# A metaformer block on one core: the written order of five work tables and the places of the reciprocals are arranged anew

## The chip, the cores and the metric

One NeuronCore of a Trainium2 chip. The metric is device time in microseconds (us) of one execution, all weights and the eight images read from HBM and the result written back. Lower is better. The kernel before: 1431.96 us, the median of three runs (1431.75, 1431.96, 1438.49).

## The reference, cut to what matters

Eight images of 256 channels x 32 x 32, float32, pass one block: a channel norm, a multi-scale linear attention with a projection and batch norm added to the input, then a token norm and a mixture of six small experts added to that. The expert weights of an image are chosen from the mean of its tokens, so no expert product can be finished before the norm of the whole image is known.

```python
qkv = conv2d(ln_c(x), qkv_w)                       # 1x1, 256 -> 768
agg = conv2d(qkv, agg_dw_w, groups=768, padding=2) # depthwise 5x5
agg = conv2d(agg, agg_pw_w, groups=96)             # 8 by 8 groups
ms = concatenate([qkv, agg], axis=1)               # 64 heads of (q, k, v), 8 each
kv = einsum('bhnd,bhne->bhde', relu(k), [v, 1])
out = einsum('bhnd,bhde->bhne', relu(q), kv)
out = out[..., :-1] / (out[..., -1:] + 1e-15)      # the reciprocals meant here
x = x + bn(conv2d(out, proj_w))                    # 512 -> 256
t = ln_t(tokens(x))
w = experts(softmax(mean(t) @ router_w.T))         # top 2 of 11 rows
t = tokens(x) + sum_e w[e] * (gelu(t @ W1[e] + b1[e]) @ W2[e] + b2[e])
```

## The kernel before, in words

A list `ORDER` of 1786 work items is built by `schedule()` from tables of words. Each engine (PE, ACT, POOL, and SyncE for the transfers) walks the same list and executes its own part of each item, in that order; semaphores hold it until the other engines' parts are done. So the position of a word in a table is the program order of that step on every engine that has a part in it. `FIRST` is image 0 up to the keys of its second attention half, `SECOND` is image 1 with the second half of image 0 beside it, `PLAN` serves the next five images, `LAST` the eighth, `END` closes. In a word, the image number is relative: `-1` is the image before.

The items that matter here, with the line of their main instruction:

- `squares` (ACT, L781), `sums` (POOL, L913 and L915), `stats` (PE, L652; ACT copies it out), `rnorm` (POOL, ending in L929), `rbc` (PE L661, ACT L864), `apply` (POOL, L935), `high` (ACT), `low` (POOL, L940): one norm of an image, a chain in this order. Its third number is 0 for the channel norm and 1 for the token norm.
- `qkv` (PE L516, six fp16 products of 128x512; ACT L823 drains it), for six tiles of 128 rows and two halves.
- `diag` (PE L586, eight float32 products with diagonal matrices that ACT makes in `matrices`) and `b` (POOL, L983 adds what ACT L742 has scaled) share the depthwise 5x5 with VectorE (DVE). `b` takes the next waiting piece, if there is one.
- DVE doesn't walk the list. It runs the taps of the 5x5 (L1190) one behind the other, tile pair 1, then 2, then 0 of each image: 108 taps in image 0, 140 in image 1, 132 in the others. `AGG_PLACES` and `RAW_PLACES` say before which tap of an image it takes up a small task: the reciprocals of the attention sums (`rden`, L1074, raw half of this image, agg half of the last) and the routing of the experts.
- `tok` (PE transposes of q, k, v; ACT L844 and L845), `kv` (PE L616), `mask` (POOL, L947 and L948), `att` (PE L628, ACT L851 and L852), `scale` (POOL L956, after `rden`), `back` (PE L635), `proj` (PE L642, ACT, POOL L1010): the attention. `agg` (PE L596, L601) is the grouped 1x1 after the taps.
- `F` is a first expert product (`ffn`, PE L516, ACT L873 with the Gelu), `G` its split in two fp16 parts (ACT L767, L768; POOL L1024), `S` the second product (PE L534). There are 32 of each for every image, and they are given only when their inputs are in the list; else the word does nothing. `F` of an image can start when both `low` of its token norm are done.

All items with a PSUM product but `S` share two banks in turn: a product may be filled when the one two places before it in the list is drained by ACT. `qkv` of a tile pair overwrites the rows that DVE reads, so ACT drains it only when the taps of the image before are done for that pair.

Of the kernel before, what the change touches and what calls it, by code (L numbers as in the profile page):

```python
# [1253 lines left out]
```

## Time and profile before

| | us |
|---|---|
| median of three runs | 1431.96 |
| the profiled execution, its own time | 1438.11 |
| its span, first to last instruction | 1436.4 |
| PE busy in it | 1355.8 |
| DVE busy | 1198.0 |
| ACT busy | 1092.1 |
| POOL busy | 1043.6 |

The profiled execution stands at the upper one of the three timed runs. "Busy" of PE includes the stretches in which its clock was granted at half speed: there the same product takes twice as long. The first image is in flight alone up to about 171 us, the second with it up to about 331 us; from there each image takes 160 us up to the last two.

### The profile page before, as it was taken

Reading aid. Unit: us, or ns where it says so; the run is one execution under the profiler, and the core shown is the slowest. Engines: PE = TensorE matmul, PEld = TensorE weight load, DVE = VectorE, ACT = ScalarE, POOL = GpSimd, SP = SyncE. Lnnn points to the kernel's source line nnn. Section 1 sums busy time; section 2 is a strip of 40 time slices with the busy share of each in tenths; the row PEclk is TensorE's granted clock in tenths of the full one; section 3 lists DMA queues with packets and bytes.
Section 4 is the critical chain, followed back from the end, with each engine's and each line's share of the span. In section 5 each row is a group of like instructions: output and inputs, shape, how many; then the busy total and the mean of one; then the engine's idle time right before and its main releaser. Section 6 shows DMA issues by size and latency. Waiting matters only on the chain.

```text
span 1436.4 us, 18823 instructions
## 1 busy us (share of the span) xinstructions
PE 1355.8 (94%) x6844; PEld 771.8 (54%) x6844; DVE 1198.0 (83%) x1248; ACT 1092.1 (76%) x1919; POOL 1043.6 (73%) x771
## 2 busy tenths in 40 slices
...
GB/s 236 30 30 30 1 30 0 1 31 15 1 1 45 44 1 1 45 30 15 1 1 44 45 1 1 45 1 16 0 3 42 16 0 1 45 15 1 16 15 15
DMA packets 14284, 32.76 MB, mean 23 GB/s; under 512 B 2416, under 2 KB 5360, under 8 KB 13936
## 3 DMA queue, kind: packets, MB, share of 16 engines
...
q14 instruction: 38, 0.31, 0.1%
...
## 4 chain that ended last, share of the span: by engine, by line
PE 82%; ACT 9%; DVE 3%; POOL 2%; issue 2%; DMA 0%; ACTq 0%; DVEq 0%; SPq 0%; POOLq 0%
PE wbk L516 30%; PE acc L534 21%; PE wbk L642 7%; PE wbk L628 4%; PE wbk L601 4%; PE wbk L652 4%; PE wbk L616 4%; DVE dacc L1190 3%; PE wbk L586 3%; PE wbk L596 2%; PE wbk L635 2%; PE wbk L609 1%; ACT hb L873 1%; PE wbk L661 1%; ACT kt L851 1%
## 5 line engine op out<-in xcount | busy, mean ns | idle before, releaser
L1190 DVE SCALAR_TENSOR_TENSOR dacc<-qkvs,dww,dacc 128x930 f32<-128x930 f32 (+4 forms) x896 | 988.0, 1183 | 0.0
L1024 POOL TENSOR_TENSOR gl<-hb,gh 128x512 f16<-128x512 f32 x256 | 304.9, 1195 | 172.5 <-ACT hb L768 170.4
L983 POOL TENSOR_TENSOR dwo<-dwo,tapb 128x960 f32<-128x960 f32 (+2 forms) x136 | 307.4, 2261 | 75.7 <-ACT tapb L742 65.3
L873 ACT ACTIVATE hb<-wbk,b1s 128x512 f32<-128x512 f32 x256 | 174.4, 684 | 93.4 <-PE wbk L516 87.3
L534 PE MATMUL acc<-gh,w2h 128*128 128x512 f16 x512 | 194.1, 379 | 1.4 <-POOL gl L1024 1.0
L534 PE MATMUL acc<-gl,w2h 128*128 128x512 f16 x512 | 194.0, 379 | 0.0
L534 PE MATMUL acc<-gh,w2l 128*128 128x512 f16 x512 | 194.0, 379 | 0.0
L767 ACT ACTIVATE gh<-hb,ew 128x512 f16<-128x512 f32 x256 | 182.9, 715 | 0.1
L768 ACT ACTIVATE hb<-hb,ew 128x512 f32<-128x512 f32 x256 | 182.5, 713 | 0.0
L516 PE MATMUL wbk<-th,w1h 128*128 128x512 f16 x512 | 152.6, 380 | 4.9 <-POOL tl L940 1.7
L742 ACT ACTIVATE tapb<-qkvs,dww 128x1024 f32<-128x1024 f32 x136 | 154.0, 1146 | 1.7 <-POOL dwo L983 1.7
L516 PE MATMUL wbk<-th,w1l 128*128 128x512 f16 x512 | 152.8, 380 | 0.0
L516 PE MATMUL wbk<-tl,w1h 128*128 128x512 f16 x512 | 152.4, 379 | 0.0
L628 PE MATMUL wbk<-kvm,qr 128*128 128x144 f32 x512 | 83.6, 302 | 12.0 <-POOL kvm L948 3.0
L628 PEld LDWEIGHTS wbk<-kvm,qr 128*128 128x128 f32 x512 | 71.0, 193 | 30.8 <-ACT den L852 12.2
L1074 DVE RECIPROCAL den<-den 128x128 f32<-128x128 f32 x32 | 30.2, 945 | 64.9 <-ACT den L852 64.9
L823 ACT ACTIVATE qkvs<-wbk 128x512 f32<-128x512 f32 x96 | 56.6, 592 | 35.0 <-PE wbk L516 33.5
L516 PEld LDWEIGHTS wbk<-tl,w1h 128*128 128x128 f16 x512 | 50.1, 98 | 60.6 <-issue 0.3
L516 PEld LDWEIGHTS wbk<-th,w1l 128*128 128x128 f16 x512 | 50.2, 98 | 60.5 <-issue 0.2
L534 PEld LDWEIGHTS acc<-gh,w2l 128*128 128x128 f16 x512 | 50.1, 98 | 60.4
L534 PEld LDWEIGHTS acc<-gh,w2h 128*128 128x128 f16 x512 | 50.2, 98 | 58.0 <-issue 3.8
L956 POOL TENSOR_TENSOR kt<-kt,den 128x1024 f32<-128x1024 f32 x32 | 63.0, 1970 | 24.9 <-DVE den L1074 24.9
...
## 6 DMA issues: line engine op xcount, KB each, us to landing
...
```

The lines of the kernel that those rows point to most:

```text
L516: last = nc.tensor.matmul(dst, w[:, k, m * P:(m + 1) * P], d[:, k, c * CH:(c + 1) * CH], start=(i == 0), stop=(i == len(parts) - 1))
L534: last = nc.tensor.matmul(acc[:, m, :], w[:, t, m * P:(m + 1) * P], d[:, f % GB, :], start=(t == 0 and i == 0), stop=(t == FT - 1 and i == 2),
L628: last = nc.tensor.matmul(b[:, g * RD:(g + 1) * RD], qr[:, g, t * P:(t + 1) * P], kvm[:, g, :], start=True, stop=True)
L642: last = nc.tensor.matmul(b[:], wp[:, k, m * P:(m + 1) * P], (ac, qr)[k // CT][:, k % CT, c * CH:(c + 1) * CH], start=(k == 0), stop=(k == ...
L742: ins = nc.scalar.activation(tapb[:, BASE_NO[s, m, i] % 2, :], qkvs[:, m, :], ACT.Copy, scale=w)
L767: nc.scalar.activation(gh[:, f % GB, :], hb[:, f % GB, :], ACT.Copy, scale=w).then_inc(g_high, 1)
L768: nc.scalar.activation(hb[:, f % GB, :], hb[:, f % GB, :], ACT.Copy, scale=w).then_inc(g_scaled, 1)
L873: last = nc.scalar.activation(hb[:, f % GB, :], b[:], ACT.Gelu, bias=b1s[:, f % FT:f % FT + 1], scale=1.0 / (X_SCALE * W_SCALE))
L956: nc.gpsimd.tensor_tensor(v, v, r, ALU.mult).then_inc(att_scaled[h], 1)
L983: ins = nc.gpsimd.tensor_tensor(d3[:, oy, ox], d3[:, oy, ox], t3[:, iy, ix], ALU.add)
L1024: nc.gpsimd.tensor_tensor(gl[:, f % GB, :], hb[:, f % GB, :], gh[:, f % GB, :], ALU.subtract).then_inc(g_low, 1)
L1190: ins = nc.vector.scalar_tensor_tensor(out=dst[:, oy, ox], in0=i3[:, jy, jx], scalar=dww[:, m, tap:tap + 1], in1=a3[:, oy, ox], op0=ALU.mu ...
```

## The change

No instruction is added or removed: the 1786 items are the same ones, and only their positions in the list differ, and with them the order of each engine's program. The taps of DVE keep their order; five of the six small tasks in image 1 and some in the others move by one to six taps. The main moves:

- `FIRST`: the first `w1h` stands before the two drains of qkv tile 3; both drains of tile 4 stand before the matrices of tile 4, and both of tile 5 before the `w2h`. In image 2's first norm, `squares`, `sums` and `stats` stand before `agg.3.1` and the four qkv of image 1, `rnorm` right behind and `rbc` after those four (before, `squares` came between the qkv, and `stats` and `rbc` stood before the last of them). The second `apply` of it stands after the first qkv of tile 4 and not at the end of the table.
- `SECOND`: `high.1.0.1` stands after the second pair of proj; `squares.-1.1` and one `b` stand before `relu_q` and `qkv.1.2.0`; both `rbc` of the token norm after `att.5`; `qkv.1.3.0` among the `back`; one `G` between the first two `F`; `squares.2.0`, `sums.2.0` before the `agg` of tile 3; `stats.2.0` one `F` later.
- `RAW_PLACES[1]` goes from (66, 71) to (64, 68), that of the middle images from (64, 69) to (62, 66), `AGG_PLACES[1]` from (21, 23, 75, 78) to (20, 23, 73, 76).
- `PLAN`, `LAST` and `END` are shuffled over short distances; the number of `F`, `G` and `S` in each stage stays within one.

```diff
--- before.py
+++ after.py
@@ -163,77 +163,77 @@
 FIRST = """
 squares.0.0.0 squares.0.0.1 sums.0.0 wqh.0 stats.0.0 rnorm.0.0 roots.0 rbc.0.0.0 rbc.0.0.1 means.0.0
 means.0.1 means.0.2 means.0.3 apply.0.0.0 apply.0.0.1 high.0.0.0 low.0.0.0 high.0.0.1 low.0.0.1 qkv.0.2.0
-qkv.0.2.1 qkv.0.3.0 qkv.0.3.1 w1h.0.0 b w1l.0.0 qkv.0.4.0 matrices.0.4 qkv.0.4.1 qkv.0.5.0 w2h.0.0 w2h.0.1
-w2l.0.0 qkv.0.5.1 squares.1.0.0 matrices.0.5 w2l.0.1 w1h.0.1 b b diag.0.4.0 diag.0.4.1 w1l.0.1 squares.1.0.1
-sums.1.0 diag.0.5.0 diag.0.5.1 b qkv.0.0.0 b matrices.0.0 qkv.0.0.1 b matrices.0.1 stats.1.0 rnorm.1.0 b
-diag.0.0.0 qkv.0.1.0 rbc.1.0.0 rbc.1.0.1 b qkv.0.1.1 b diag.0.0.1 apply.1.0.0 apply.1.0.1 high.1.0.0 b
-diag.0.1.0 tok.0.0 b b tok.0.1 b b diag.0.1.1 b low.1.0.0 tok.0.2 tok.0.3 high.1.0.1 tok.0.4 b tok.0.5
-tok.0.6 tok.0.7 b relu_q.0.0 b kv.0.0.0 kv.0.0.1 mask.0.0 relu_q.0.1 att.0.0.0 att.0.0.1 b att.0.0.2
-att.0.0.3 scale.0.0.0 att.0.0.4 att.0.0.5 att.0.0.6 att.0.0.7 scale.0.0.1 back.0.0.0.0 back.0.0.0.1
-back.0.0.1.0 back.0.0.1.1 agg.0.2.0 agg.0.2.1 agg.0.3.0 b low.1.0.1 b agg.0.3.1 b qkv.1.2.0 squares.2.0.0
-squares.2.0.1 sums.2.0 qkv.1.2.1 qkv.1.3.0 stats.2.0 rnorm.2.0 rbc.2.0.0 rbc.2.0.1 qkv.1.3.1 agg.0.4.0
-agg.0.4.1 agg.0.5.0 apply.2.0.0 b agg.0.5.1 qkv.1.4.0 qkv.1.4.1 qkv.1.5.0 qkv.1.5.1 b b kv.0.1.0 kv.0.1.1 b
-mask.0.1 b b apply.2.0.1
+qkv.0.2.1 w1h.0.0 w1l.0.0 qkv.0.3.0 qkv.0.3.1 qkv.0.4.0 qkv.0.4.1 matrices.0.4 qkv.0.5.0 qkv.0.5.1 w2h.0.0
+w2h.0.1 w2l.0.0 matrices.0.5 w2l.0.1 w1h.0.1 diag.0.4.0 diag.0.4.1 squares.1.0.0 w1l.0.1 b squares.1.0.1 b b
+b sums.1.0 diag.0.5.0 b diag.0.5.1 qkv.0.0.0 matrices.0.0 b qkv.0.0.1 matrices.0.1 b stats.1.0 b diag.0.0.0
+diag.0.0.1 rnorm.1.0 rbc.1.0.0 b rbc.1.0.1 b apply.1.0.0 qkv.0.1.0 qkv.0.1.1 b b apply.1.0.1 high.1.0.0 b
+tok.0.0 diag.0.1.0 b b diag.0.1.1 tok.0.1 tok.0.2 low.1.0.0 high.1.0.1 tok.0.3 b b tok.0.4 tok.0.5 tok.0.6
+tok.0.7 b relu_q.0.0 kv.0.0.0 b kv.0.0.1 mask.0.0 relu_q.0.1 att.0.0.0 b att.0.0.1 b att.0.0.2 att.0.0.3
+scale.0.0.0 att.0.0.4 att.0.0.5 att.0.0.6 att.0.0.7 scale.0.0.1 back.0.0.0.0 back.0.0.0.1 back.0.0.1.0
+back.0.0.1.1 b agg.0.2.0 agg.0.2.1 agg.0.3.0 low.1.0.1 squares.2.0.0 squares.2.0.1 sums.2.0 stats.2.0
+agg.0.3.1 rnorm.2.0 qkv.1.2.0 qkv.1.2.1 qkv.1.3.0 qkv.1.3.1 rbc.2.0.0 rbc.2.0.1 b agg.0.4.0 agg.0.4.1
+apply.2.0.0 agg.0.5.0 agg.0.5.1 qkv.1.4.0 apply.2.0.1 qkv.1.4.1 qkv.1.5.0 qkv.1.5.1 b b kv.0.1.0 kv.0.1.1 b
+mask.0.1 b b
 """.split()
 
 SECOND = """
-agg.-1.0.0 G F agg.-1.0.1 agg.-1.1.0 S agg.-1.1.1 att.-1.1.0 S G b att.-1.1.1 att.-1.1.2 att.-1.1.3 S
-scale.-1.1.0 att.-1.1.4 F b qkv.0.0.0 G att.-1.1.5 S att.-1.1.6 att.-1.1.7 scale.-1.1.1 S qkv.0.0.1
-qkv.0.1.0 back.-1.1.0.0 G back.-1.1.0.1 back.-1.1.1.0 back.-1.1.1.1 qkv.0.1.1 b S proj.-1.0.0 proj.-1.0.1 b
-F high.1.0.0 low.1.0.0 high.1.0.1 proj.-1.1.0 proj.-1.1.1 F G low.1.0.1 b tok.0.0 tok.0.1 G F S tok.0.2
-tok.0.3 F tok.0.4 G tok.0.5 F b tok.0.6 tok.0.7 b b qkv.1.2.0 F relu_q.0.0 squares.-1.1.0 squares.-1.1.1
-kv.0.0.0 kv.0.0.1 sums.-1.1 b mask.0.0 relu_q.0.1 stats.-1.1 rnorm.-1.1 S att.0.0.0 G G b att.0.0.1
-att.0.0.2 G att.0.0.3 scale.0.0.0 rbc.-1.1.0 F S att.0.0.4 att.0.0.5 att.0.0.6 S rbc.-1.1.1 att.0.0.7
-apply.-1.1.0 apply.-1.1.1 qkv.1.2.1 scale.0.0.1 F high.-1.1.0 back.0.0.0.0 S back.0.0.0.1 G high.-1.1.1 b S
-back.0.0.1.0 F low.-1.1.0 low.-1.1.1 logits.-1 back.0.0.1.1 exp.-1 qkv.1.3.0 qkv.1.3.1 G agg.0.2.0 F F
-squares.2.0.0 F F agg.0.2.1 b squares.2.0.1 sums.2.0 agg.0.3.0 agg.0.3.1 G G S G stats.2.0 F rnorm.2.0 F G G
-S F S G b F agg.0.4.0 b S F S b G rbc.2.0.0 S G rbc.2.0.1 b apply.2.0.0 S F F S S G agg.0.4.1 G F agg.0.5.0
-S S G agg.0.5.1 qkv.1.4.0 b F b kv.0.1.0 F G G S G qkv.1.4.1 S b F S F G qkv.1.5.0 apply.2.0.1 qkv.1.5.1 S G
-b b F S F G G F S S G b F S kv.0.1.1 F mask.0.1 b G b S
+S G G F S agg.-1.0.0 agg.-1.0.1 agg.-1.1.0 agg.-1.1.1 att.-1.1.0 F b att.-1.1.1 att.-1.1.2 S att.-1.1.3 G S
+scale.-1.1.0 att.-1.1.4 att.-1.1.5 att.-1.1.6 b qkv.0.0.0 att.-1.1.7 qkv.0.0.1 F qkv.0.1.0 scale.-1.1.1 G
+back.-1.1.0.0 back.-1.1.0.1 back.-1.1.1.0 back.-1.1.1.1 F F proj.-1.0.0 S qkv.0.1.1 proj.-1.0.1 b high.1.0.0
+F b low.1.0.0 G proj.-1.1.0 proj.-1.1.1 high.1.0.1 low.1.0.1 G b G tok.0.0 tok.0.1 F tok.0.2 b S tok.0.3
+tok.0.4 b tok.0.5 S tok.0.6 tok.0.7 squares.-1.1.0 squares.-1.1.1 S b G relu_q.0.0 qkv.1.2.0 kv.0.0.0
+sums.-1.1 b F kv.0.0.1 mask.0.0 relu_q.0.1 stats.-1.1 rnorm.-1.1 b att.0.0.0 G S att.0.0.1 att.0.0.2 G
+att.0.0.3 scale.0.0.0 S att.0.0.4 att.0.0.5 rbc.-1.1.0 rbc.-1.1.1 apply.-1.1.0 att.0.0.6 att.0.0.7 S F G F F
+apply.-1.1.1 scale.0.0.1 qkv.1.2.1 back.0.0.0.0 high.-1.1.0 qkv.1.3.0 b back.0.0.0.1 high.-1.1.1 S G
+low.-1.1.0 low.-1.1.1 logits.-1 back.0.0.1.0 back.0.0.1.1 exp.-1 qkv.1.3.1 agg.0.2.0 F G S F F squares.2.0.0
+squares.2.0.1 sums.2.0 S agg.0.2.1 agg.0.3.0 agg.0.3.1 b F G G G F stats.2.0 G rnorm.2.0 S F F G F rbc.2.0.0
+agg.0.4.0 b S F S G b G S G rbc.2.0.1 b S F S agg.0.4.1 F G S agg.0.5.0 G F S G agg.0.5.1 qkv.1.4.0 F b S S
+F apply.2.0.0 b S b F G kv.0.1.0 b qkv.1.4.1 G G S qkv.1.5.0 F apply.2.0.1 G qkv.1.5.1 b S F F S b G G F S G
+b S kv.0.1.1 mask.0.1 F S F S G b b
 """.split()
 
 PLAN = """
-agg.-1.0.0 F agg.-1.0.1 S G agg.-1.1.0 agg.-1.1.1 S att.-1.1.0 att.-1.1.1 att.-1.1.2 F G qkv.0.0.0 qkv.0.0.1
-S G att.-1.1.3 scale.-1.1.0 att.-1.1.4 att.-1.1.5 att.-1.1.6 att.-1.1.7 scale.-1.1.1 qkv.0.1.0 b qkv.0.1.1
-high.1.0.0 F F back.-1.1.0.0 G S back.-1.1.0.1 F b back.-1.1.1.0 G b low.1.0.0 S back.-1.1.1.1 S proj.-1.0.0
-b b high.1.0.1 low.1.0.1 G proj.-1.0.1 proj.-1.1.0 F tok.0.0 tok.0.1 tok.0.2 tok.0.3 tok.0.4 tok.0.5 tok.0.6
-b b tok.0.7 b proj.-1.1.1 F relu_q.0.0 kv.0.0.0 squares.-1.1.0 squares.-1.1.1 sums.-1.1 kv.0.0.1 F mask.0.0
-relu_q.0.1 S G stats.-1.1 att.0.0.0 att.0.0.1 rnorm.-1.1 S G att.0.0.2 att.0.0.3 rbc.-1.1.0 rbc.-1.1.1
-apply.-1.1.0 G apply.-1.1.1 scale.0.0.0 att.0.0.4 F att.0.0.5 att.0.0.6 att.0.0.7 G qkv.1.2.0 scale.0.0.1
-high.-1.1.0 high.-1.1.1 S low.-1.1.0 F qkv.1.2.1 back.0.0.0.0 S b low.-1.1.1 logits.-1 back.0.0.0.1
...
+agg.-1.0.0 F agg.-1.0.1 agg.-1.1.0 agg.-1.1.1 G S att.-1.1.0 att.-1.1.1 att.-1.1.2 G F b qkv.0.0.0 S G
+qkv.0.0.1 att.-1.1.3 scale.-1.1.0 S att.-1.1.4 att.-1.1.5 att.-1.1.6 att.-1.1.7 scale.-1.1.1 b qkv.0.1.0 F
+qkv.0.1.1 high.1.0.0 F back.-1.1.0.0 G S back.-1.1.0.1 back.-1.1.1.0 b G S F S back.-1.1.1.1 G F low.1.0.0
+high.1.0.1 proj.-1.0.0 b proj.-1.0.1 b low.1.0.1 proj.-1.1.0 tok.0.0 tok.0.1 tok.0.2 tok.0.3 tok.0.4 tok.0.5
+tok.0.6 b tok.0.7 b proj.-1.1.1 F relu_q.0.0 kv.0.0.0 squares.-1.1.0 squares.-1.1.1 sums.-1.1 F kv.0.0.1 b
+mask.0.0 G relu_q.0.1 S stats.-1.1 rnorm.-1.1 att.0.0.0 att.0.0.1 S G att.0.0.2 att.0.0.3 rbc.-1.1.0
+rbc.-1.1.1 apply.-1.1.0 apply.-1.1.1 G scale.0.0.0 att.0.0.4 F att.0.0.5 att.0.0.6 att.0.0.7 scale.0.0.1 G
+high.-1.1.0 S qkv.1.2.0 high.-1.1.1 F qkv.1.2.1 back.0.0.0.0 b low.-1.1.0 low.-1.1.1 S logits.-1
...
-AGG_PLACES = {1: (21, 23, 75, 78), 2: (16, 18, 79, 85), 7: (22, 27, 84, 88), 8: (19, 21, 75, 83)}
-RAW_PLACES = {0: (82, 83), 1: (66, 71), 2: (64, 69), 7: (76, 78)}
+AGG_PLACES = {1: (20, 23, 73, 76), 2: (17, 18, 75, 85), 7: (19, 25, 85, 88), 8: (19, 21, 75, 83)}
+RAW_PLACES = {0: (82, 83), 1: (64, 68), 2: (62, 66), 7: (70, 76)}
```

## Rows read from the trace of the kernel before

**Rows 1.** The page: the span, and busy us, share and instructions per engine

```profile
span 1436.4 us, 18823 instructions
PE 1355.8 (94%) x6844; PEld 771.8 (54%) x6844; DVE 1198.0 (83%) x1248; ACT 1092.1 (76%) x1919; POOL 1043.6 (73%) x771
```

**Rows 2.** Windows: stretch, length, busy us per engine, PE clock, DMA share, GB/s

```profile
124.00:171.00 47.00, 38.43 (x233) 30.35 (x234) 42.97 (x44) 21.06 (x45) 18.26 (x15) 0.89 0.00 1
214.00:254.80 40.80, 26.86 (x158) 19.92 (x158) 40.33 (x50) 24.49 (x52) 34.16 (x23) 0.87 0.00 0
272.60:331.00 58.40, 57.33 (x297) 30.38 (x295) 58.40 (x56) 49.28 (x75) 48.23 (x35) 1.00 0.07 24
491.00:651.00 160.00, 158.27 (x837) 91.66 (x837) 150.36 (x156) 134.87 (x236) 130.56 (x97) 1.00 0.06 20
1131.00:1436.40 305.40, 288.26 (x1407) 151.70 (x1406) 145.42 (x167) 214.34 (x382) 174.10 (x138) 0.99 0.03 13
```

**Rows 3.** Waits of PE, 60 to 272.6 us: total us, times, longest

```profile
PE wbk L635 <- POOL kt L956: 9.0, 3, 5.5
...
PE wbk L661 <- POOL sv L929: 3.1, 1, 3.1
...
PE wbk L652 <- POOL rb L913: 2.7, 1, 2.7
```

**Rows 4.** The chain that ended last, 195 to 262 us: start, length, what

```profile
223.50 13.06 DVE dacc L1190 x12
236.56 0.86 DVE den L1074
...
237.49 1.97 POOL kt L956
239.46 4.39 POOL nrm L935 x2
...
244.05 1.97 POOL kt L956
...
246.16 1.09 PE wbk L635 x4
...
249.05 5.02 PE wbk L516 x12
...
257.64 2.76 PE wbk L516 x12
```

**Rows 5.** Timeline of DVE: start, us, operation, idle before and its releaser

```profile
130.09 0.95 DVE L1074 RECIPROCAL den<-den 128x128 f32<-128x128 f32 x1 [2.96 <-ACT den L852]
...
183.65 0.95 DVE L1074 RECIPROCAL den<-den 128x128 f32<-128x128 f32 x1 [0.70 <-ACT den L852]
...
187.62 0.95 DVE L1074 RECIPROCAL den<-den 128x128 f32<-128x128 f32 x1 [0.87 <-ACT den L852]
...
218.72 4.77 DVE L1179 SCALAR_TENSOR_TENSOR dacc<-qkvs,dww,dwo 128x1024 f32<-128x1024 f32 x2
...
319.99 3.60 DVE L1179 SCALAR_TENSOR_TENSOR dacc<-qkvs,dww,dwo 128x1024 f32<-128x1024 f32 x2
...
344.76 0.95 DVE L1074 RECIPROCAL den<-den 128x128 f32<-128x128 f32 x1 [5.86 <-ACT den L852]
```

**Rows 6.** Timeline of PE: starts of qkv.0.5.1, kv, the first F, agg.1.0.0

```profile
43.44 0.61 PE L516 MATMUL wbk<-xh,wqh 128*128 128x512 f16 x2 [1.33 <-ACT qkvs L823]
...
117.87 5.17 PE L616 MATMUL wbk<-vt,kt 128*128 128x129 f32 x32 [0.84 <-ACT vt L845]
...
254.79 0.59 PE L516 MATMUL wbk<-th,w1h 128*128 128x512 f16 x2
...
327.91 1.02 PE L596 MATMUL wbk<-dwo,pw 128*128 128x512 f32 x2
```

**Rows 7.** Timeline of POOL: the first sum of image 0's token norm, its two low

```profile
219.12 3.28 POOL L913 TENSOR_TENSOR rb<-yr 128x1024 f32<-128x1024 f32 x1
...
248.56 4.21 POOL L940 TENSOR_TENSOR tl<-nrm,th 128x1024 f16<-128x1024 f32 x2
```

More of the change, by code:

```diff
@@ new lines @@
+high.-1.1.0 S qkv.1.2.0 high.-1.1.1 F qkv.1.2.1 back.0.0.0.0 b low.-1.1.0 low.-1.1.1 S logits.-1
+back.0.0.0.1 back.0.0.1.0 G qkv.1.3.0 b F back.0.0.1.1 b S qkv.1.3.1 agg.0.2.0 agg.0.2.1 squares.2.0.0
+squares.2.0.1 agg.0.3.0 F S exp.-1 agg.0.3.1 F sums.2.0 S G G F G stats.2.0 F S b G F rnorm.2.0 F G S F F G
+S rbc.2.0.0 b G S agg.0.4.0 F b S agg.0.4.1 G S rbc.2.0.1 b F agg.0.5.0 S G G agg.0.5.1 G qkv.1.4.0 S F b F
+F apply.2.0.0 G S b qkv.1.4.1 qkv.1.5.0 G b S G F b S S F F G S G S apply.2.0.1 G F qkv.1.5.1 S G F F G b b
@@ L209 @@
+S G F S b kv.0.1.0 G S kv.0.1.1 b mask.0.1 F b S
 """.split()
 LAST = """
[L212 to L216 removed]
@@ L217 @@
-rnorm.-1.1 att.0.0.0 att.0.0.1 G b S F rbc.-1.1.0 F rbc.-1.1.1 apply.-1.1.0 apply.-1.1.1 G att.0.0.2 F
-att.0.0.3 scale.0.0.0 att.0.0.4 S att.0.0.5 att.0.0.6 att.0.0.7 high.-1.1.0 b S F high.-1.1.1 S F low.-1.1.0
-low.-1.1.1 logits.-1 G G F scale.0.0.1 back.0.0.0.0 G back.0.0.0.1 F b back.0.0.1.0 S back.0.0.1.1 agg.0.2.0
-S exp.-1 S b G agg.0.2.1 agg.0.3.0 F agg.0.3.1 G G G S F S G b b b F S S F S S G F G b G agg.0.4.0 F G S S F
-S G F F b agg.0.4.1 b agg.0.5.0 F G S G agg.0.5.1 S b G F S S G F F F G S S G F b F G S G S G kv.0.1.0
```

36 lines of the change are left out of this document (18 added, 18 removed).

## The prediction, made before the changed kernel ran

> **What bounds the kernel now.** First the page [rows 1]: PE is busy 1355.8 of 1436.4 us, so all its idle time is 80.6 us, and since the change keeps every instruction, that and the time lost at the half clock is all that there is to win. Then the windows [rows 2], for where the idle time lies. An image of the middle (491 to 651) takes 160.0 us with 1.73 us idle: no order gains more than that there. The two last images (1131 to 1436.4) hold 17.1 us. The stretch from 124 to 254.8 us is the soft one: 8.6 idle of 47.0 in 124 to 171, 13.9 of 40.8 in 214 to 254.8, and in both the granted clock is 0.89 and 0.87, a mix of 2.4 GHz and 1.2 GHz. From 272.6 on PE is nearly full (1.1 idle of 58.4), with expert products to fill every hole. So the end is the moment at which PE becomes full, plus a fixed amount of PE work: what brings image 0's token norm, and with it the first F at 254.79 [rows 6], forward, brings the end forward.
>
> Then the waits of PE in that stretch [rows 3]: 9.0 us for the scaled attention (L635 from POOL L956, one of 5.5), 3.1 for a norm factor (L661), 2.7 for a sum (L652). And the chain that ended last [rows 4], to see what is behind them: it runs over the taps of DVE (1.09 us each: 13.06 over 12), then the reciprocal at 236.56, POOL's scale at 237.49, its two apply (4.39), its second scale at 244.05, and PE's back at 246.16. That is, POOL waits for a reciprocal that stands behind taps, and the apply and the second scale queue behind the first. After it PE runs twelve products of qkv in 5.02 us at half clock where twelve F products take 2.76 a little later, and DVE has no idle time between 188.5 and 339 us but its small tasks.
>
> **The change part by part.** The sum is for the profiled execution: 1438.11 us, its span 1436.4 and 1.7 around it. It stands 6.15 above the median.
>
> *FIRST, up to kv.0.0.* `w1h` (1.9 us of ACT) now lies in ACT's wait for the qkv of tile 3, both drains of tiles 4 and 5 precede longer work, so the 1.33 us wait of qkv.0.5.1 [rows 6] and a smaller one go. PE is about 2.3 us ahead into the `diag`; of that ACT takes back some at the eight `tok`, which it drains at over 0.5 us each with a `high` and two `b` among them. I get kv.0.0 at 116.2 instead of 117.87 [rows 6]: 1.65 us. Ends: 0 (ACT's `b` eat all) and 2.5. DVE gains the same, because its first reciprocal waited 2.96 us for the attention [rows 5]; if nothing were gained before, it would still wait that.
>
> *Image 2's first norm.* `stats` and `rbc` now lie around four qkv (5.2 us of PE at full clock), which covers `rnorm`, so the 3.1 us wait for L929 [rows 3] and half a us before it go. In its place `stats` stands ahead of `agg.3.1`, and its second half needs POOL's second sum, which needs both `squares`, which ACT now does behind the drain of `agg.3.0`. I walk that to a wait of about 3.1 us. Net 0.5 gained; ends -1 and 3, the latter if the half clock that lies on `rbc` and qkv there (0.89 in the window) moves off too. The second `apply` (2.37 us of POOL) moves into a long idle time of POOL, and no longer stands between `b` and `scale`; it was covered there, so 0.
>
> *SECOND, to the first scale.* The reciprocals of image 0's second half waited 0.70 and 0.87 us [rows 5], so one place earlier costs DVE nothing as long as PE moves forward with it, and may save those two waits: DVE is 2.1 to 3.2 us ahead after them. `squares` off the drain of qkv.1.2.0, which waits for taps, gives ACT back 1.4 us and starts them 8 us earlier, but POOL's sum at 219.12 [rows 7] was queued behind four `b`, of which one now has to wait for the `squares`; I put the sum at 217 and the second sum 3 us ahead. Then the deciding edit: `RAW_PLACES[1]` 66 to 64 takes two taps, 2.2 us, out of the chain in front of the first scale, and 71 to 68 three out of the second. With DVE's own 2.1 to 3.2 that makes 4.3 to 5.4 us on POOL's scale at 237.49. What is late next is the attention product: its fourth drain, 3 us ahead as well, gets there at about 229.3, which allows up to 7.2. I take 6. Both `rbc` are one and two `att` later, and the `apply` still fit between the two scales. So back.1 and logits come 6 us sooner, and POOL's two `low` end at 246.5 instead of 252.77 [rows 7].
>
> One place where the page and the trace can be put side by side: DVE's two first taps of a tile pair (L1179, two inputs in SBUF) took 4.77 us [rows 5] while POOL's sum took 3.28 [rows 7], against 2.5 and 2.4 elsewhere. The Trainium skill (SBUF — State Buffer, "Who interferes with whom") has it that a DVE instruction with two SBUF inputs and a GpSimd one that reads SBUF lock each other out of a shared port. By that the later sum against the earlier taps would part them, and DVE would have 2.3 us more; the sum above does without.
>
> *To the first F and after.* Before, the first F came 2.0 us after `low`, behind four qkv groups' worth of products at half clock (5.02, [rows 4]). Now qkv.1.3.0 fills the wait for the second scale and only one qkv and one agg remain behind logits, so F starts with `low`: 246.5 against 254.79, a gain of 8.3, that is, 6.0 and 2.3 more. Then the 2.7 us wait of `stats` for POOL's sum [rows 3], which stood behind a `b`, goes; in its place ACT has a G before the second F's Gelu and two `squares` before it can drain `agg.2.1`, on which `agg.3.1` waits; I count about 2.2 lost again. Net 0.5; ends -2 and 3. Sum so far: 8.3 + 0.5 = 8.8 us (the 1.65 and 0.5 of the first parts are in the 6).
>
> *Does DVE allow it?* agg.1.0.0 starts at 327.91 [rows 6], its taps are done where DVE begins the next image, at 319.99 [rows 5]: 7.9 us of slack. PE moves 8.8 and DVE at least 2, so about 1 or more is left. DVE's next wait (5.86, [rows 5]) absorbs the difference. If DVE gained nothing, 7.9 would be the cap.
>
> *PLAN, LAST, END.* Short shuffles, with places of reciprocals moved by up to six taps. The rows bound them: below by 1.73 us idle per image of the middle, five of them, and about 12 of the last 17.1 us (over 4 are the drain and the store at the end). Upward, one new wait like those of the first images (0.7 to 3.1) per image would cost 3 to 15. The number of F in LAST is one less ahead of its token norm. I take 0.
>
> Sum: 8.8 us. 1438.11 - 8.8 = 1429.3 for such an execution. The runs at 1431.8 may lack a part of the half-clock time that the profiled one has; of the 5.02 us above, 2.3 would be missing there. For the median I take 8 us: 1424.0.
>
> The other side of the clock: in 214 to 254.8 it was granted at 0.87 with 13.9 us idle, and the products behind the idle time ran at 1.2 GHz. After the change PE still idles some 6 us in front of the first F. The Trainium skill (TensorE: Matmul & The Clock Gate, "What's actually happening") says that the clock is halved after an idle window and given back after a busy one. By that the half clock stays and lies on F, which nothing hides.
>
> **The rivals.** (a) *The half clock falls on F.* For: the wait before F doesn't vanish. The same length of slow products as before (5.02 us) moves to F; the 2.3 us that I gain there is gone: 5.5 to 6.5 us, 1426. (b) *The gain before PE is full is used up by DVE.* The waits of the reciprocals only move: DVE is dense, and if FIRST gives nothing and the first two places wait 1.1 us longer each, scale.0 comes 2.2 us sooner and no more. Against: 2.96 us of wait in image 0 are PE's doing. 3 us gained: 1429. (c) *The tables of the middle lose it.* PLAN runs five times; one new wait of 2 to 3 us in it (a `kv` that now stands at the very end, its mask straight before the next image's `att`) costs 10 to 15, and with 8 gained it turns the sign from 1.6 us per image on: slower by 4, 1436. Against: the order in the rest of PLAN is close to the old one, and ACT (134.9 of 160) and POOL (130.6) have room [rows 2]. (d) *LAST and END gain too.* 17.1 us idle; a third of it, 5, makes 1419.
>
> **How the numbers follow.** Forecast 0.45, (a) 0.15, (b) 0.12, (c) 0.10, (d) 0.18. The forecast's own range is 1420 to 1427. With (a), (b) and (d) whole and half of (c), the range is 1415 to 1433. A half per cent is 7.2 us, about what a measurement of this kernel tells from no change: faster means under 1424.8. (d) is, the forecast is to some seven tenths (its centre is 0.8 under the line), a tenth of the rest: 0.18 + 0.31 + 0.03 = 0.52. Slower than 1439.1 takes more than (c) in its middle: 0.06. The rest, 0.42, is within.
>
> **What would show it.** Reciprocal of image 1 (L1074) at about 230 instead of 236.5 and no 5.5 us wait of L635 behind it; the first F at 245 to 248; the wait for L929 at 151 us gone and one for L915 or L781 in its place; kv.0.0 near 116; windows of 160 us in the middle unchanged. Wrong if F starts before 249 and the span doesn't follow, or if an image of the middle takes over 161 us.

## The result, and the profile after

The changed kernel took 1422.66 us, the median of five runs (1418.52 to 1424.02), beside 1431.96 for the kernel before: ratio 0.9913, 95% interval 0.9886 to 0.9940. Timed again later beside more runs of the kernel before, it was 0.9903 (0.9875 to 0.9930). The forecast was 1424.0, range 1415 to 1433. The total came out; its parts did not, and that is what the experiments are about.

One thing must be known to read the numbers: the executions of the kernel before fall into two groups, near 1432 (clock mostly 0.990 to 0.992 over the span) and near 1438.7 (0.985 to 0.988). In the series of e1 to e4 below, 14 of its 35 runs were in the lower one. The profiles of before and after are both of the kind with more half clock (0.986 each), so they differ by 14.1 us where the first medians differ by 9.3.

The page of the kernel after, its answer to [rows 1]:

```profile
span 1422.3 us, 18823 instructions
PE 1350.7 (95%) x6844; PEld 775.6 (55%) x6844; DVE 1197.5 (84%) x1248; ACT 1091.6 (77%) x1919; POOL 1038.3 (73%) x771
```

Its windows (columns as in [rows 2]):

```profile
124.00:171.00 47.00, 39.49 (x234) 32.27 (x235) 40.20 (x40) 21.29 (x46) 20.00 (x16) 0.85 0.07 23
214.00:254.80 40.80, 31.63 (x198) 22.53 (x197) 39.87 (x54) 31.13 (x62) 34.90 (x24) 0.96 0.00 0
272.60:331.00 58.40, 57.32 (x286) 30.12 (x286) 58.40 (x53) 48.22 (x73) 46.78 (x34) 0.99 0.07 28
```

In 214 to 254.8, PE is busy 31.6 us instead of 26.9: there the early gain is. In 124 to 171 the clock is even lower than before, 0.85, and DVE is busy 40.2 instead of 43.0. The places where PE passes the first product of `agg.s.0.0` (L596), and the starts of kv.0.0 and of the first F, read from both timelines, say what each stage gave between these two executions:

| start of | before | after | gained so far |
|---|---|---|---|
| kv.0.0 | 117.87 | 114.48 | 3.4 |
| agg.0.0.0 | 170.82 | 170.40 | 0.4 |
| first F | 254.79 | 248.49 | 6.3 |
| agg.1.0.0 | 327.91 | 323.11 | 4.8 |
| agg.2.0.0 | 488.60 | 483.42 | 5.2 |
| agg.5.0.0 | 968.77 | 961.61 | 7.2 |
| the end | 1436.4 | 1422.3 | 14.1 |

So a third of it comes before 331 us, not all; 2.4 us in the stages of the middle and 6.9 from 969 on. The rows before 331 us hold for these two executions only. A second profile of the same changed kernel (e5 below, 1418.94 us) has agg.0.0.0 at 162.38, the first F at 245.01 and agg.1.0.0 at 317.85, 8.0, 3.5 and 5.3 us ahead of the first one. Behind agg.1.0.0 the two agree: 1099.2 and 1099.4 us to the end, where the kernel before takes 1108.5. So 9.3 us of the gain lie there in both, and it is the opening that differs from one execution to the next.

The waits of PE from 60 to 272.6 us, the answer to [rows 3]:

```profile
PE wbk L609 <- ACT vt L845: 6.9, 7, 2.0
PE wbk L628 <- POOL kvm L948: 3.9, 1, 3.9
PE wbk L652 <- POOL nrm L915: 3.4, 2, 3.2
PE wbk L665 <- ACT th L752: 2.9, 1, 2.9
PE wbk L601 <- DVE dwo L1173: 2.7, 1, 2.7
```

The 5.5 us for the second scale and the wait for L929 have gone; the one for the second sum (3.2) has come as forecast, and two are new, 2.9 in front of logits and 2.7 for DVE's taps. The largest sum, the waits of `tok` for ACT's drains (L609), was 4.0 before. DVE's timeline:

```profile
129.83 0.95 DVE L1074 RECIPROCAL den<-den 128x128 f32<-128x128 f32 x1 [5.64 <-ACT den L852]
...
182.89 0.95 DVE L1074 RECIPROCAL den<-den 128x128 f32<-128x128 f32 x1 [1.20 <-ACT den L852]
...
218.09 2.49 DVE L1179 SCALAR_TENSOR_TENSOR dacc<-qkvs,dww,dwo 128x1024 f32<-128x1024 f32 x2
...
231.89 0.95 DVE L1074 RECIPROCAL den<-den 128x128 f32<-128x128 f32 x1 [0.43 <-ACT den L852]
...
342.35 0.95 DVE L1074 RECIPROCAL den<-den 128x128 f32<-128x128 f32 x1 [1.05 <-ACT den L852]
```

The first wait grew from 2.96 to 5.64, so DVE gained 0.3 us there and not 1.65; the 5.86 of slack at 339 is nearly used up. The two first taps of the tile pair at 218 us took 2.49 us instead of 4.77: POOL's sum, which ran beside them before, now starts at 219.91, when they are nearly done. POOL's timeline from 219 to 249, the answer to [rows 4, 7]:

```profile
219.91 2.89 POOL L913 TENSOR_TENSOR rb<-yr 128x1024 f32<-128x1024 f32 x1
...
231.26 2.30 POOL L983 TENSOR_TENSOR dwo<-dwo,tapb 128x992 f32<-128x992 f32 x1
233.52 1.97 POOL L956 TENSOR_TENSOR kt<-kt,den 128x1024 f32<-128x1024 f32 x1
235.44 4.68 POOL L935 TENSOR_TENSOR nrm<-yr,rb 128x1024 f32<-128x1024 f32 x2
240.07 1.97 POOL L956 TENSOR_TENSOR kt<-kt,den 128x1024 f32<-128x1024 f32 x1
244.17 4.21 POOL L940 TENSOR_TENSOR tl<-nrm,th 128x1024 f16<-128x1024 f32 x2
```

Both scales come 4.0 us sooner, though the sum comes 0.8 later. The first reciprocal is done at 232.84, and the scale then stands behind a `b` (L983) to 233.5: 0.7 us of what DVE gained is lost there. Two `low` end at 248.4 and F follows at 248.49.

### The profile page after: what moved, and what is told of

Same layout as the page of the kernel before. It is cut to its first block, busy times and chain, and to the rows that moved or that the text cites. A ratio compares the mean times of both kernels' runs of the same rounds, so it can differ in the third digit from the quotient of the medians.

```text
span 1422.3 us, 18823 instructions
## 1 busy us (share of the span) xinstructions
PE 1350.7 (95%) x6844; PEld 775.6 (55%) x6844; DVE 1197.5 (84%) x1248; ACT 1091.6 (77%) x1919; POOL 1038.3 (73%) x771
## 4 chain that ended last, share of the span: by engine, by line
PE 82%; ACT 9%; POOL 3%; DVE 3%; issue 2%; DMA 0%; DVEq 0%; SPq 0%; ACTq 0%; POOLq 0%
PE wbk L516 28%; PE acc L534 21%; PE wbk L642 8%; PE wbk L628 4%; PE wbk L601 4%; PE wbk L616 4%; PE wbk L586 4%; PE wbk L652 3%; DVE dacc L1190 2%; PE wbk L596 2%; PE wbk L635 1%; PE wbk L609 1%; ACT kt L851 1%; PE wbk L661 1%; POOL gl L1024 1%
## 5 line engine op out<-in xcount | busy, mean ns | idle before, releaser
L1190 DVE SCALAR_TENSOR_TENSOR dacc<-qkvs,dww,dacc 128x930 f32<-128x930 f32 (+4 forms) x896 | 988.0, 1183 | 0.0
L1024 POOL TENSOR_TENSOR gl<-hb,gh 128x512 f16<-128x512 f32 x256 | 300.3, 1175 | 176.7 <-ACT hb L768 174.1
L983 POOL TENSOR_TENSOR dwo<-dwo,tapb 128x960 f32<-128x960 f32 (+2 forms) x136 | 307.7, 2262 | 46.8 <-ACT tapb L742 41.6
L873 ACT ACTIVATE hb<-wbk,b1s 128x512 f32<-128x512 f32 x256 | 174.3, 684 | 81.9 <-PE wbk L516 75.4
L534 PE MATMUL acc<-gh,w2h 128*128 128x512 f16 x512 | 194.3, 380 | 1.8 <-POOL gl L1024 1.0
L534 PE MATMUL acc<-gl,w2h 128*128 128x512 f16 x512 | 194.3, 379 | 0.0
L534 PE MATMUL acc<-gh,w2l 128*128 128x512 f16 x512 | 194.2, 379 | 0.0
L516 PE MATMUL wbk<-th,w1h 128*128 128x512 f16 x512 | 152.4, 379 | 3.1 <-ACT hb L873 1.4
L516 PE MATMUL wbk<-tl,w1h 128*128 128x512 f16 x512 | 152.3, 379 | 0.0
L516 PE MATMUL wbk<-th,w1l 128*128 128x512 f16 x512 | 152.3, 379 | 0.0
L534 PEld LDWEIGHTS acc<-gh,w2l 128*128 128x128 f16 x512 | 50.1, 98 | 60.5 <-issue 0.3
L516 PEld LDWEIGHTS wbk<-tl,w1h 128*128 128x128 f16 x512 | 50.1, 98 | 60.4
L516 PEld LDWEIGHTS wbk<-th,w1l 128*128 128x128 f16 x512 | 50.1, 98 | 60.4
L534 PEld LDWEIGHTS acc<-gh,w2h 128*128 128x128 f16 x512 | 50.3, 98 | 55.8 <-issue 3.2
L534 PEld LDWEIGHTS acc<-gl,w2h 128*128 128x128 f16 x512 | 50.1, 98 | 53.5 <-issue 2.5
```

What stands on the lines that cost most here:

```text
L516: last = nc.tensor.matmul(dst, w[:, k, m * P:(m + 1) * P], d[:, k, c * CH:(c + 1) * CH], start=(i == 0), stop=(i == len(parts) - 1))
L534: last = nc.tensor.matmul(acc[:, m, :], w[:, t, m * P:(m + 1) * P], d[:, f % GB, :], start=(t == 0 and i == 0), stop=(t == FT - 1 and i == 2),
L873: last = nc.scalar.activation(hb[:, f % GB, :], b[:], ACT.Gelu, bias=b1s[:, f % FT:f % FT + 1], scale=1.0 / (X_SCALE * W_SCALE))
L983: ins = nc.gpsimd.tensor_tensor(d3[:, oy, ox], d3[:, oy, ox], t3[:, iy, ix], ALU.add)
L1024: nc.gpsimd.tensor_tensor(gl[:, f % GB, :], hb[:, f % GB, :], gh[:, f % GB, :], ALU.subtract).then_inc(g_low, 1)
L1190: ins = nc.vector.scalar_tensor_tensor(out=dst[:, oy, ox], in0=i3[:, jy, jx], scalar=dww[:, m, tap:tap + 1], in1=a3[:, oy, ox], op0=ALU.mu ...
```

## The experiments

### One table at a time (e1 to e4)

Each is the kernel before with one part of the change, the words exactly those of the diff (here only the names of what is taken over):

```diff
 e1: +FIRST     e2: +SECOND, +AGG_PLACES[1], +RAW_PLACES[1]
 e3: +PLAN, +AGG_PLACES[2], +RAW_PLACES[2]     e4: +LAST, +END, +AGG_PLACES[7], +RAW_PLACES[7]
```

> The kernel before with the new FIRST alone. Theory A (the prediction's): the attention of image 0 comes 1.65 us sooner and image 2's first norm saves half a us more; DVE goes with it, so about 2 us are gained in the end, 1430. Theory B (read from the two traces, agg.0.0.0 at 170.8 before and 170.4 after): the 3.4 us that kv.0.0 comes sooner are lost again in the wait for the mask (3.9 us) and in half clock before 171 us, so 0 to 0.5 us are gained, 1432.

> The kernel before with the new SECOND and the places of image 1 alone. Theory A: the larger part of the forecast's 8.8 us is here, 6 to 7 us, 1425 to 1426. Theory B: of the 6.3 us by which the first F comes sooner, 1.5 are lost again behind it (a wait of 2.7 us of agg.1.4.0 for the taps of DVE), so 4 to 4.5 us, 1427.5; agg.1.0.0 starts at about 323.5.

> The kernel before with the new PLAN and the places of the images 2 to 6 alone. Theory A: 0 us (1432). Theory B: the step from agg to agg of an image goes from 160.05 to 159.4 us, five images, about 2.8 us, 1429. Rival C: the new PLAN gains only where SECOND hands over earlier, and alone its steps stay at 160.0.

> The kernel before with the new LAST and END and the places of the images 7 and 8 alone. Theory A: 0 us. Theory B: 157.2 + 154.6 us from agg.6.0.0 to the end become about 150.9 + 151.8, of which 2.6 are work that the new PLAN has done before; so 5 to 6.5 us, 1426 to 1427: most of what the change gains beside SECOND, and a part for which the prediction had put 0.

| kernel | ratio to before | 95% interval | median us, 12 runs |
|---|---|---|---|
| e1, FIRST | 0.9978 | 0.9959 to 0.9997 | 1434.22 |
| e2, SECOND | 0.9956 | 0.9935 to 0.9976 | 1430.93 |
| e3, PLAN | 0.9975 | 0.9953 to 0.9997 | 1429.98 |
| e4, LAST and END | 0.9950 | 0.9931 to 0.9970 | 1428.61 |

(before: 1437.19, 35 runs.) A median of the kernel before depends on how many runs fall in each group, so read the ratios. Each part gains by itself, e1 and e3 only just clear of 1. For e1 (0.22 per cent, about 3 us) the interval takes in theory A's 2 us and not theory B's 0 to 0.5. For e2 (0.44, about 6) it takes in both theories. Theory A gave 0 to the last two, and is wrong there: together they are over half. Theory B said 2.8 us for e3 and 5 to 6.5 for e4; the traces show 2.6 and 6.6 behind agg.1.0.0. In e3 the steps of the middle (from one image's first agg product to the next one's) are 159.40 us, as in the whole change, also behind the old SECOND; so rival C falls. The same stretch in both kernels, agg.2.0.0 to agg.3.0.0, first e3:

```profile
482.50:641.90 159.40, 157.71 (x837) 92.05 (x837) 150.14 (x155) 134.46 (x238) 130.26 (x97) 1.00 0.06 21
```

and the kernel before:

```profile
488.60:648.70 160.10, 158.37 (x838) 91.76 (x837) 150.46 (x157) 134.96 (x237) 130.66 (x97) 1.00 0.06 20
```

PE's idle time is the same 1.7 us; it is the busy time that fell by 0.66. The gain is in how closely the products follow each other, which the bound from idle time (1.73 per image) did not look at. The idle weight-load time put down to issue in front of L516 and L534 fell from 2.8 to 1.7 us; why just these orders do so stays open.

In e4 the steps from agg.5 to the end are 158.4, 150.9 and 151.8 (before: 155.8, 157.2, 154.6). The waits of PE in LAST, first of the kernel before, 1124 to 1282 us:

```profile
PE wbk L516 <- POOL tl L940: 1.7, 1, 1.7
PE wbk L616 <- ACT vt L845: 1.5, 1, 1.5
PE wbk L516 <- ACT kt L838: 1.0, 1, 1.0
PE wbk L661 <- ACT hb L873: 0.8, 1, 0.8
```

and of e4, 1119 to 1271 us:

```profile
PE wbk L516 <- ACT hb L873: 1.1, 2, 0.7
PE wbk L516 <- POOL tl L940: 0.8, 1, 0.8
PE wbk L628 <- ACT qr L836: 0.8, 1, 0.8
```

Three waits of 1.5, 1.0 and 0.8 us go and the one for `low` halves; 1.1 us for Gelu drains (L873) come. The kernel before has a half clock stretch of 3.4 us behind its wait for `low`, in 1196 to 1216 (mean granted clock there 0.91), and e4 has none. That stretch isn't in every execution of the old LAST: e1, e2, e6 and e7 have the same wait at full clock and a step of 156.1 instead of 157.2. So some 1.1 of the 6.6 us that e4's trace gains behind agg.1.0.0 is the clock, and 5.5 the order. With e3's 2.6 the 6.6 make 9.2, the 9.3 us of the whole change behind agg.1.0.0: these two parts add up.

e1's timeline has agg.0.0.0 at 166.49, 4.3 us before the kernel before, and e3 and e4, whose FIRST and SECOND are the old ones, have agg.1.0.0 at 322.2 and 320.4 instead of 327.9. So one execution cannot tell a gain of this size in the first 330 us: the same order lands up to 7.5 us apart. In 100 to 141 us the granted clock was 0.88 in the profile of before and 1.00 in those of e3 and e4. Only like can be set beside like: with more half clock agg.1.0.0 goes from 327.91 to 323.11 (4.8 us); with little of it, from 322.2 and 320.4 (e3, e4) to 317.85 (e5), 2.5 to 4.4 us. For kv.0.0 the mean of the six profiles with the new FIRST is 115.3, of the seven with the old one 116.9: 1.5 us, not the 3.4 of the table above.

### The whole again, the places, and the waits filled (e5 to e8)

e5 is the changed kernel again. e6 is e2 without its places. e7 is the kernel before with the places alone:

```diff
-AGG_PLACES = {1: (21, 23, 75, 78), ...
-RAW_PLACES = {..., 1: (66, 71), ...
+AGG_PLACES = {1: (20, 23, 73, 76), ...
+RAW_PLACES = {..., 1: (64, 68), ...
```

e8 is the changed kernel and, on PE, in front of four items:

```diff
+            FILLERS = {('att', 0, 0, 0): 12, ('back', 0, 0, 1, 0): 6, ('kv', 0, 0, 0): 2, ('logits', 0): 12}
...
+                    for i in range(FILLERS[it]):
+                        nc.tensor.matmul(acc[:, 0, :], w1h[:, 0, 0:P], w1h[:, 0, 0:CH], start=True, stop=True,
+                                         skip_group_check=True)
```

> The changed kernel itself, timed in the same series as the parts: the runs of the kernel before fall into two groups here, near 1432 and 1438.7, and its first five runs were nearly all of the lower one. Theory A (the prediction's 8 to 9 us, all before 331 us): 0.9940. Theory B (the parts add up: FIRST 0.2, SECOND 0.4, PLAN 0.25, LAST and END 0.5 per cent): about 0.987 to 0.988, 1424 where before is 1437.

> The kernel before with the new SECOND, but the places of the reciprocals of image 1 left as they were. Theory A: the places are the deciding edit of SECOND, scale.1.0.0 waits for the reciprocal behind tap 66 again, and 2 to 4 of SECOND's 6 us go: 0.997 to 0.9985. Theory B: the order of PE and ACT does it, 0.996 as with the places.

> The kernel before with the places of image 1 alone (RAW 64, 68; AGG 20, 23, 73, 76), all tables old. Theory A: the first scale comes about 2 us sooner, the second 2 to 3, back.1 with it, 2 us gained: 0.9985. Theory B: without the order that lets the attention product come sooner the reciprocal only waits: 0 (1.000).

> The changed kernel with 32 products more on PE that nothing reads (fp16, 128x512 into the still unused acc), put into four waits of image 0 and its token norm: 12 before att.0.0.0, 6 before back.0.0.1.0, 2 before kv.0.0.0, 12 before logits.0, 7 us of PE at full clock. Theory D: the two groups of times come from stretches at 1.2 GHz that follow PE's waits before 250 us; work in the waits holds 2.4 GHz, so the upper group goes and the median falls 2 to 4 us below the changed kernel's. Theory E: the groups have another cause, or the filling delays what it stands before: the same as the changed kernel or up to 5 us slower.

| kernel | ratio to before | 95% interval | median us (runs) |
|---|---|---|---|
| e5, the change | 0.9903 | 0.9875 to 0.9930 | 1421.59 (6) |
| e6, SECOND, old places | 0.9966 | 0.9947 to 0.9986 | 1431.67 (12) |
| e7, places alone | 0.9976 | 0.9953 to 0.9998 | 1430.79 (12) |
| e8, the change, waits filled | 0.9879 | 0.9851 to 0.9907 | 1416.48 (6) |

(before: 1437.33, 23 runs.) e5 lies between the two theories: theory A's 0.9940 is outside its interval, theory B's 0.988 inside. The places gain 0.24 per cent with all tables old, 3.4 us; the interval takes in theory A's 2 and ends just below 1. The traces speak more clearly against theory B, that the reciprocal would only wait. In e3, whose first two images are those of the kernel before, and e7 the first reciprocal of image 0 stands at 125.95 and 126.17, the clock is 1.00 up to 141 us in both, and then e7 has the scales of image 1 at 229.61 and 236.15 instead of 231.78 and 238.34, 2.2 us sooner each, which is two taps, and agg.1.0.0 1.5 sooner. SECOND's order without them gains 0.34, with them 0.44; the last two intervals overlap, so how much they add to it isn't told. The chain of [rows 4] was read rightly. The parts multiply to 0.986 and the whole is 0.990: the parts overlap by some 6 us, or less: 0.986 lies just below the whole's interval, and each part is known to 0.002 only.

e8 is the fastest kernel here, by work that nobody reads: 5 us under the changed one by the medians, 3.3 by the means of six runs each. Five of its runs lie in 1416.0 to 1418.2 and one at 1422.67, so the slower kind of execution became rarer and did not go.

### Why two groups, and where the early gain ends (e9 to e11)

e9 moves one word in SECOND of the changed kernel:

```diff
-agg.0.4.0 b S F S G b G S G rbc.2.0.1 ...
+b S F S agg.0.4.0 G b G S G rbc.2.0.1 ...
```

e10 is the kernel before with `FILLERS = {('att', 0, 0, 0): 12, ('back', 0, 0, 1, 0): 6, ('kv', 0, 0, 0): 2, ('back', 1, 0, 1, 0): 20}`. e11 is e8 with e9's word moved and `('stats', 2, 0): 12, ('agg', 0, 1, 0): 10` besides.

> The changed kernel with one word of SECOND moved: agg.0.4.0 (for image 1, agg.1.4.0) stands two products of F and S later, behind the piece b S F S. In the changed kernel PE waits 2.7 us at this word for the taps of DVE. Theory B: that wait is part of where the early gain goes; it shrinks to nothing and the kernel gains 1 to 2.7 us, agg.1.0.0 sooner by as much. Rival: DVE is what bounds this stretch, the wait comes back at the next thing that needs its taps (agg.1.4.1, the qkv of tile 4), 0 us.

> The kernel before, all tables and places old, with 40 products more on PE that nothing reads, in the same four waits of image 0 and its token norm (12 before att.0.0.0, 6 before back.0.0.1.0, 2 before kv.0.0.0, 20 before back.1.0.1.0). Theory D: the two groups of the kernel before (1432 and 1438.7) are the half clock between 115 and 140 us and its consequences; the upper group disappears, the median is 1429 to 1432, 0.994 to 0.996. Theory E: two groups as before, ratio 1.000 or above.

> The changed kernel with agg.0.4.0 later and the filling products of e8, and 22 more of them (12 before stats.2.0, where PE waits 3 us for the second sum, 10 before agg.0.1.0, where it waits 2.5 for ACT). Theory D with B: both gains add, 1413 to 1416, 2 us under e8, and the half clock at 141 and 168 us goes. Rival: these two waits lie beside DVE's taps and aren't on the path, and the filling delays them: as e8, 1416.5, or 1 us above.

The series of e9 to e11 has 17 runs of the kernel before, median 1432.63. e10: 0.9969 (0.9951 to 0.9987), median 1431.22, and its 12 runs lie between 1428.84 and 1433.41; of the 17 runs beside it, 8 were at 1437.2 and above. The upper group is gone, the lower one hardly faster: theory D, though its 0.994 to 0.996 was a little more than was found. The stretch 100 to 141 us, first the kernel before as profiled:

```profile
100.00:141.00 41.00, 30.97 (x151) 23.21 (x150) 36.97 (x37) 23.10 (x51) 29.00 (x18) 0.88 0.16 52
```

the kernel after:

```profile
100.00:141.00 41.00, 30.10 (x142) 24.38 (x141) 34.20 (x34) 20.24 (x47) 26.79 (x16) 0.79 0.15 52
```

and e10:

```profile
100.00:141.00 41.00, 36.01 (x198) 24.42 (x197) 39.15 (x39) 26.23 (x56) 27.09 (x17) 0.96 0.15 52
```

The same stretch in e5, which is the same program as the kernel after:

```profile
100.00:141.00 41.00, 28.83 (x168) 22.01 (x167) 39.43 (x38) 23.58 (x51) 27.86 (x17) 0.96 0.15 52
```

PE's rows say what happens, first the kernel before, then the kernel after:

```profile
126.08 6.51 PE L628 MATMUL wbk<-kvm,qr 128*128 128x144 f32 x32 [3.04 <-POOL kvm L948]
```

```profile
114.48 6.77 PE L616 MATMUL wbk<-vt,kt 128*128 128x129 f32 x32 [0.85 <-ACT vt L845]
125.11 7.32 PE L628 MATMUL wbk<-kvm,qr 128*128 128x144 f32 x32 [3.86 <-POOL kvm L948]
```

then e5, with its first reciprocal:

```profile
115.02 5.38 PE L616 MATMUL wbk<-vt,kt 128*128 128x129 f32 x32 [0.85 <-ACT vt L845]
122.41 5.18 PE L628 MATMUL wbk<-kvm,qr 128*128 128x144 f32 x32 [2.00 <-POOL kvm L948]
125.49 0.95 DVE L1074 RECIPROCAL den<-den 128x128 f32<-128x128 f32 x1 [0.91 <-ACT den L852]
```

and e3, the old opening with the clock at 1.00:

```profile
116.79 3.81 PE L616 MATMUL wbk<-vt,kt 128*128 128x129 f32 x32 [0.84 <-ACT vt L845]
122.62 5.17 PE L628 MATMUL wbk<-kvm,qr 128*128 128x144 f32 x32 [2.02 <-POOL kvm L948]
```

The clock falls to 1.2 GHz a first time in front of the mask, at `kv`, behind PE's short waits for ACT's drains at `tok` (0.50 in 114 to 120 us of the kernel after). What the slow kv sets off is told by the four short pieces of the mask on POOL (L947, L948) and DVE's two first taps of the next tile pair (L1179):

| profile | mask on POOL | it takes | DVE's two taps start | PE's wait for the mask | att |
|---|---|---|---|---|---|
| before | 123.54 | 2.4 | 124.62 | 3.04 | 6.51 |
| after | 121.75 | 3.3 | 121.50 | 3.86 | 7.32 |
| e5 | 120.90 | 1.4 | 122.05 | 2.00 | 5.18 |
| e3 | 121.10 | 1.4 | 123.55 | 2.02 | 5.17 |

Where a piece of the mask starts with these taps running it takes 1.1 to 1.4 us instead of 0.3 to 0.5. That is so in before, after, e1, e2, e6 and e9, and there the att products run in half clock for most of their time (6.2 to 7.4 us). In e3, e4, e5, e7, e8, e10 and e11 the last piece starts ahead of the taps, in e5 by 0.03 us, and att takes 5.1 to 5.2. So a small delay at kv decides between two times that lie far apart: the mask meets the taps, PE waits longer for it, the clock falls again, the reciprocals come later, and DVE, which has no slack before 339, loses for good what it waits: the fourth figure of the windows is its busy time, 37.0, 34.2 and 39.2 of 41 us, and 39.4 in e5. From before to e3 this can be added up. DVE's waits for the attention sums up to 190 us are 5.6 and 0.9 us, a difference of 4.7; e3 was ahead by 1.1 at 124 us; together that is, to 0.1, the 5.7 us between their starts of image 2's taps (319.99 and 314.29) and between their agg.1.0.0. That the order of these steps is cause and effect is read from the rows; no run parts the mask from the taps. Why the same order keeps the full clock at kv in one execution and not in another no run here shows.

In e10 the twelve products fill the mask's wait:

```profile
116.98 4.92 PE L627 MATMUL wbk<-vt,kt 128*128 128x129 f32 x32
121.75 2.75 PE L546 MATMUL acc<-w1h 128*128 128x512 f16 x12
124.33 5.10 PE L639 MATMUL wbk<-kvm,qr 128*128 128x144 f32 x32
```

The att products took 7.32 us in the kernel after and take 5.10 here. The kv of e10 is still in half clock for a part (4.92), but its mask is clear of the taps; so the 12 products and the clear mask come together, and which of them holds the clock isn't told. The Trainium skill (TensorE: Matmul & The Clock Gate, "HAM oscillation — how this bites in real kernels") describes such a drop behind waits, there for transfers; the trace agrees that it falls behind waits, and has what it costs one engine further: between before and e3 kv and att are 2.7 us longer, and agg.1.0.0 comes 5.7 us later; the two groups stand 6.6 apart.

e9: 0.9907 (0.9879 to 0.9936), 1421.55: no different from e5. The wait of 2.7 us is gone, agg.1.0.0 starts at 319.82, 3.3 us sooner than in the first profile of the change, and the next image takes 164.5 us instead of 160.3. In e9:

```profile
319.80:484.40 164.60, 157.62 (x832) 91.26 (x832) 164.10 (x165) 135.45 (x239) 132.44 (x94) 1.00 0.06 20
```

DVE is busy 164.1 of 164.6: it is the bound of that image. Its rows for the start of the last tile pair of image 1 and for its first taps of image 2 are these, in e9:

```profile
270.87 4.49 DVE L1179 SCALAR_TENSOR_TENSOR dacc<-qkvs,dww,dwo 128x1024 f32<-128x1024 f32 x2
...
319.59 3.79 DVE L1179 SCALAR_TENSOR_TENSOR dacc<-qkvs,dww,dwo 128x1024 f32<-128x1024 f32 x2
```

and in the kernel after:

```profile
271.08 2.49 DVE L1179 SCALAR_TENSOR_TENSOR dacc<-qkvs,dww,dwo 128x1024 f32<-128x1024 f32 x2
...
317.79 5.17 DVE L1179 SCALAR_TENSOR_TENSOR dacc<-qkvs,dww,dwo 128x1024 f32<-128x1024 f32 x2
```

In e9 PE came to agg.1.0.0 at the moment at which its taps were done, and these were done 1.8 us later than in the kernel after. The two taps at 271 us took 2.0 us longer. The moved word lets the `b` that stood behind agg.1.4.0 go first, and POOL's part of it (L983, 2.3 us) runs at 270.79, over these two taps, instead of at 275.11, behind them.

e11 with its 22 products more takes 1421.54 (0.9915, 0.9886 to 0.9943), 5 us above e8, though the intervals of the two ratios overlap. Its granted clock is 0.991 to 0.998 over the span, that of e8 0.990 to 0.995: no less full clock, and nothing won by it. In e11 PE is at agg.1.0.0 at 315.01, in e8 at 315.09, but the step behind it is 164.5 in e11 and 160.3 in e8. DVE begins image 2 here, first e8:

```profile
264.48 2.49 DVE L1190 SCALAR_TENSOR_TENSOR dacc<-qkvs,dww,dwo 128x1024 f32<-128x1024 f32 x2
...
311.18 4.18 DVE L1190 SCALAR_TENSOR_TENSOR dacc<-qkvs,dww,dwo 128x1024 f32<-128x1024 f32 x2
```

then e11:

```profile
266.06 4.49 DVE L1190 SCALAR_TENSOR_TENSOR dacc<-qkvs,dww,dwo 128x1024 f32<-128x1024 f32 x2
...
314.77 3.80 DVE L1190 SCALAR_TENSOR_TENSOR dacc<-qkvs,dww,dwo 128x1024 f32<-128x1024 f32 x2
```

So an opening at 315 is no limit by itself. In e5, e8, e9 and e11 agg.2.0.0 comes 164.2 to 164.8 us behind DVE's first tap of image 2, wherever agg.1.0.0 was, and in the profiles of all these and of the kernel after the rest takes the same 938.9 us. DVE is 3.6 us later in e11 than in e8. 2.0 of them are the taps at 266 us, as in e9, which has the moved word and none of the filling; the first taps of the pair before, at 211.87, took 3.62 us instead of 2.49, which is 1.1 more. Whether the word alone would cost e8 this much wasn't run apart.

## Why the prediction was right, and where it was not

**The total** (1424.0 against 1422.66) was right, within the forecast's own range. **The mechanism of the first two images** was right: no 5.5 us wait behind the reciprocal of image 1 (it is there in before, e3 and e4, and 2.1 and 3.0 at most in the two profiles of the change), the wait for L929 replaced by one for L915. The places of time that were named came out as well, the reciprocal at 231.89 (said: about 230) and F at 248.49 (245 to 248), but they prove little: e4, with the old opening, has the reciprocal at 228.97 and F at 247.26. e7 shows the places as a cause of their own. Rival (a) did not come: F runs at full clock (0.59 us for two products at 248.49) and the half clock lies on the qkv in front of it (1.04 to 1.06).

**FIRST** had about the right size at kv.0.0 (1.65 said, 1.5 between the means of all profiles; the 3.4 of the table is one pair of executions). What failed is "DVE gains the same". In the first profile of the change kv took 6.77 us and the mask's wait was 3.9, in half clock, and DVE's wait rose by 2.7 to 5.64. In e5, the same program, it was 0.91. I had priced the half clock only in front of F, as rival (a), and not in front of the first reciprocal, where it decides 5 to 7 us.

**To the first F and after**, 8.8 us was mis-sized: 6.3 at F and 4.8 at agg.1.0.0 in the first pair. The scale came 4.0 us sooner, not 6. The 6 had no row under it: my own terms gave 4.3 to 5.4 for the reciprocal, and the attention product at 229.3 only allowed more. Even the 4.0 came by other terms. DVE's own advance was 0.8 at 183 us and 0.6 at 218 instead of 2.1 to 3.2. The two taps at 218 us gave 2.3, which the sum had done without, and two places their 2.2; a new wait of the reciprocal took 0.4 and POOL's `b` 0.7. The 2.7 us behind F is agg.1.4.0 (1.7 in e5), which the new table puts ahead of the end of its taps; the walk ended before it. "Does DVE allow it?" was the right question, and DVE did move by the 2.2 us it was given at least (319.99 to 317.79). What was missing is that from there on DVE, and not PE, sets when the next image is ready, once its 5.86 us of slack is gone: that is rival (b) in part.

**PLAN, LAST, END** at 0 was wrong: 2.4 and 6.9 us of 14.1. The bounds had room for it (17.1 us of idle time in the last images), and rival (d), 1419 at a chance of 0.18, was the nearer one. For PLAN the prediction's own test, windows of 160 us unchanged, failed: 159.4. My bound of 1.73 us per image and the first sentence, that idle time and half clock are all there is to win, left out that the busy time itself can fall. That both errors cancel is luck. So is the base: the kernel before had four of its first five runs in the lower group, which makes the gain between the first medians 9.3 us; beside more runs it is about 1 per cent, 14 us.
